# A postnorm layer with a routed mixture of experts on one core: the router's logits by four column groups, an earlier turn of y, one more root by bits, and ScalarE as the one that empties the shared expert's output

## What is computed

```python
def reference(x, ...):                       # x: 4 sequences of 1024 tokens of 128 values
    x = _layernorm(x + attn(x))              # a memory layer: cumulative sums of cos and sin features
    x = _layernorm(x + ffn(x))

def attn(x):
    ...                                      # den, num_re, num_im: cumsum over the 1024 positions
    y = silu(out_re * ... + out_im * ...)
    return y @ W_out

def ffn(x):                                  # flat: 4096 tokens
    logits = flat @ router_w.T               # 8 experts
    topk_p, topk_i = top_k(softmax(logits), 2)
    combine[...] = topk_p / topk_p.sum()
    for e in range(8):
        out += mlp(flat, w_fc[e], w_proj[e]) * combine[:, e]
    out += mlp(flat, shared_fc, shared_proj)     # mlp: square(relu(x @ w_fc.T)) @ w_proj.T, 512 wide
```

## Time and profile before

| | |
|---|---|
| median of 3 runs | 523.81 us (523.81 to 528.99) |
| the profiled execution | 521.17 us, of which the span of the trace 519.4 us |
| mean granted clock of TensorE | 0.963 of full speed |
| busy, of the span | PE 89%, DVE 70%, ACT 68%, POOL 56% |
| memory stage | to 232.5 us |
| dispatch stage | 232.5 to 350.2 us |
| routed stage | 350.2 to 494 us |
| POOL's 64 scatters | 234.2 to 342.4 us |

### The profile page before, as it was taken

One profiled execution on the slowest core, in us unless ns is written; L12 is line 12 of the kernel. 1 busy time (PEld: TensorE's weight loads), 2 busy tenths in 40 slices (PEclk: granted clock), 3 DMA queues, 4 the chain that ended last, 5 costly groups with the idle time before them and its releaser, 6 DMA issues.

```text
span 519.4 us, 7568 instructions
## 1 busy us (share of the span) xinstructions
PE 462.2 (89%) x2192; PEld 299.7 (58%) x2192; DVE 362.2 (70%) x843; ACT 354.0 (68%) x551; POOL 292.5 (56%) x248
## 2 busy tenths in 40 slices
PE   8897999999999988878597877869999999999984
PEld 4333344443333333446375655658999999899732
DVE  7887999999999999997667715354343334465246
ACT  3889799999999999816244625516767666566507
POOL 3473667877787778827565563521545455655400
PEclk9997999999999999999698987989999999999998
DMA  7031226664343433001111010121222221222095
GB/s 261 3 108 55 82 76 208 221 237 146 124 147 124 147 125 145 3 1 44 41 42 42 32 51 17 42 77 42 69 77 78 67 67 57 59 62 60 16 319 166
DMA packets 41192, 48.55 MB, mean 93 GB/s; under 512 B 5616, under 2 KB 25266, under 8 KB 41152
## 3 DMA queue, kind: packets, MB, share of 16 engines
q1 hardware_dynamic: 35792, 39.07, 23.0%
q0 software_dynamic: 5216, 8.70, 5.3%
q10 hardware_dynamic: 144, 0.31, 0.2%
HBM read 19.17 MB, written 29.11 MB: 93 GB/s over the span
## 4 chain that ended last, share of the span: by engine, by line
PE 36%; DVE 36%; issue 9%; ACT 8%; another core or an unknown queue 5%; POOL 3%; DMA 2%; DVEq 0%; SPq 0%; POOLq 0%; ACTq 0%
PE routed_ph L1438 13%; PE routed_po L1451 12%; DVE memory_y_raw L753 9%; DVE memory_prod L744 9%; DVE memory_feat L729 4%; PE memory_nsum L596 3%; POOL table_scratch L1129 2%; PE routed_px L1426 2%; ACT finish_xo L1645 2%; PE dispatch_spo L960 1%; ACT memory_feat L376 1%; PE dispatch_sph L950 1%; DVE dispatch_xrow L1197 1%; DMA finish_pick<-pick_scratch 1%
## 5 line engine op out<-in xcount | busy, mean ns | idle before, releaser
L479 POOL TENSOR_TENSOR memory_feat<-memory_feat,memory_p_tok 128x1024 f32<-128x1024 f32 x64 | 121.8, 1934 | 46.2 <-ACT memory_feat L387 45.2
L596 PE MATMUL memory_nsum<-memory_feat,tri 128*128 128x512 f32 x256 | 116.9, 599 | 6.6 <-ACT memory_last_rows L396 3.6
L1414 POOL DMA_INDIRECT pick_scratch<-routed_ob,routed_xg x71 | 71.3, 1005 | 78.0 <-DVE routed_ob L1535 57.7
L1129 POOL DMA_INDIRECT table_scratch<-dispatch_xrow,dispatch_slot x64 | 61.8, 966 | 47.9 <-DVE dispatch_slot L1232 25.8
L596 PEld LDWEIGHTS memory_nsum<-memory_feat,tri 128*128 128x128 f32 x256 | 47.5, 191 | 65.3 <-issue 54.5
L1484 ACT ACTIVATE routed_rel<-routed_ph 128x512 f32<-128x512 f32 x71 | 42.3, 597 | 47.5 <-PE routed_ph L1438 46.3
L1438 PE MATMUL routed_ph<-routed_xs,routed_w1c 128*128 128x256 f32 (+1 forms) x368 | 71.2, 337 | 2.1 <-ACT routed_xs L1475 1.3
L1451 PE MATMUL routed_po<-routed_w2c,routed_hid 128*128 128x128 f32 x568 | 71.2, 275 | 0.5 <-ACT routed_hid L1493 0.5
L1535 DVE TENSOR_SCALAR routed_ob<-routed_po,routed_xg 128x128 f32<-128x128 f32 x71 | 22.6, 348 | 68.9 <-issue 47.4
L744 DVE TENSOR_TENSOR memory_prod<-memory_nsum,memory_query 128x1024 f32<-128x1024 f32 x58 | 68.3, 1215 | 1.0 <-PE memory_nsum L596 1.0
L1451 PEld LDWEIGHTS routed_po<-routed_w2c,routed_hid 128*128 128x128 f32 x568 | 67.0, 192 | 0.9 <-ACT routed_hid L1493 0.7
(11 more groups left out here) (188 smaller groups left out, 652.8 us busy)
## 6 DMA issues: line engine op xcount, KB each, us to landing
table_scratch<-memory_blank SPq DMA_DIRECT2D x68, 260.0 KB, 2.6
finish_pick<-pick_scratch SPq DMA_DIRECT2D x16, 256.0 KB, 5.8
routed_xg<-table_scratch SPq DMA_DIRECT2D x25, 130.0 KB
w<-w_up SPq DMA_DIRECT2D x9, 256.0 KB, 2.7
w<-w_down SPq DMA_DIRECT2D x9, 256.0 KB, 3.2
x_tok<-x SPq DMA_DIRECT2D x4, 512.0 KB, 3.7
out<-finish_xo SPq DMA_DIRECT2D x7, 256.0 KB, 2.3
routed_xg<-table_scratch SPq DMA_DIRECT2D x21, 65.0 KB
```

Of the source, the lines that this page charges most:

```text
L479: nc.gpsimd.tensor_tensor(v, v, pv, ALU.mult).then_inc(wfeat_done, 1)
L596: last = nc.tensor.matmul(nsum[:, o:o + 512], tri[:], feat[:, i % U, h, q * 512:(q + 1) * 512], start=True, stop=True)
L1129: nc.gpsimd.indirect_dma_start(out=table, in_=xrow[:, r, n, :], in_offset=None, out_offset=bass.IndirectOffsetOnAxis(ap=slot[:, r, n:n + 1 ...
L1414: nc.gpsimd.indirect_dma_start(out=pick_dram, in_=ob[:, u, h, :], in_offset=None, out_offset=bass.IndirectOffsetOnAxis(ap=xg[:, t % XU, h, ...
```

## The change

Five edits.

- **Router.** For groups 1 to 7 the router's weights, padded with zeros from 8 to 32 columns, become the stationary side, once for each of four column groups of the PE array, and a tile of x is the moving side. The logits come out with the experts along the partitions (`plT`). ACT copies them to `lT` (new step `keep_l`, 128x128), PE turns them back by one transpose (new step `turn_l`) into `plt`, and `choose` reads them there. The logits of group 0 are made as before. The three views `plT`, `plt` and `pr` share one bank.
- **y sooner.** `turn_y(g+3)` moves from behind `up(g, 3)` to right behind `rank(g+1)`; `keep_y(g+3)` moves from ACT's end of the round to the place before `relu(g, 2)`.
- **First downs.** `down(0, 0)` and `down(0, 1)` move from ahead of `rank(1)` into round 1, where the other rounds have theirs.
- **Root of group 6** by bits instead of POW.
- **Shared output.** ACT copies `spo` to `y_all` (`keep_shared`, at the head of its round, groups 6 and 7 at the stage's end); the add of x is done on DVE in the routed stage, after tiles 6, 8, ... 20 (`add_input`), from SBUF. The finish waits for it (`summed`).

```diff
-POWERS = (0, 1, 2, 4, 6)
+POWERS = (0, 1, 2, 4)
...
-        routerT = sb("routerT", [P, E])
+        routerT = sb("routerT", [P, K])
...
+            nc.vector.memset(routerT[:, E:], 0.0)
...
-        pl, pr = plr[:, 0:GT * E], plr[:, GT * E:2 * GT * E + E]
+        plT, plt, pr = plr[:, 0:P], plr[:, P:2 * P], plr[:, 2 * P:2 * P + GT * E + E]
+        pl = plt.rearrange("p (t e) -> p t e", t=GT)[:, :, 0:E]
...
                 for t in range(GT):
-                    last = nc.tensor.matmul(pl[:, t * E:(t + 1) * E], x1T[:, g % XR, t, :], routerT[:],
-                                            start=True, stop=True)
-                last.then_inc(log_done, 1)
+                    if g:
+                        last = nc.tensor.matmul(plT[t * K:(t + 1) * K, :], routerT[:], x1T[:, g % XR, t, :],
+                                                start=True, stop=True)
+                    else:
+                        last = nc.tensor.matmul(pl[:, t, :], x1T[:, g % XR, t, :], routerT[:, 0:E], start=True, stop=True)
+                last.then_inc(routed_done if g else log_done, 1)
+
+            def turn_l(g):
+                pe.wait_ge(lT_kept, g)
+                nc.tensor.transpose(plt, lT[:], ident[:]).then_inc(log_done, 1)
...
                     up(g, 0)
                     if g + 1 < NG:
                         route(g + 1)
-                    if g > 1:
-                        down(g - 1, 0)
+                    down(g - 1, 0)
+                    if g + 1 < NG:
+                        turn_l(g + 1)
                     up(g, 1)
-                    if g > 1:
-                        down(g - 1, 1)
+                    down(g - 1, 1)
                     if g + 1 < NG:
                         rank(g + 1)
                     else:
                         total()
+                    if g + 3 < NG:
+                        turn_y(g + 3)
                     up(g, 2)
                     down(g - 1, 2)
                     up(g, 3)
-                    if g + 3 < NG:
-                        turn_y(g + 3)
                     down(g - 1, 3)
...
+            def keep_l(g):
+                act.wait_ge(routed_done, g)
+                nc.scalar.copy(lT[:], plT).then_inc(lT_kept, 1)
+
...
+            def keep_shared(g):
+                act.wait_ge(down_done, g + 1)
+                nc.scalar.copy(y_all[:, group(g), :].rearrange("p t c -> p (t c)"), spo[:]).then_inc(added, 1)
...
                 for g in range(NG):
+                    if g >= 2:
+                        keep_shared(g - 2)
                     if 0 < g < NG - 1:
                         keep_x(g + 1)
                     relu(g, 0)
+                    if 0 < g < NG - 1:
+                        keep_l(g + 1)
                     square(g, 0)
...
                         weigh(g + 1)
+                    if 0 < g and g + 3 < NG:
+                        keep_y(g + 3)
                     relu(g, 2)
...
-                    if g + 3 < NG:
-                        keep_y(g + 3)
+                    if g == 0:
+                        keep_y(3)
+                keep_shared(NG - 2)
+                keep_shared(NG - 1)
...
                 for g in range(NG):
-                    if g >= 2:
-                        add_shared(g - 2)
                     if g + 2 < NG:
                         residual(g + 2)
...
+            def add_input(g):
+                v = slice(g * GT, (g + 1) * GT)
+                dve.wait_ge(dis.added, g + 1)
+                nc.vector.tensor_tensor(y_all[:, v, :], y_all[:, v, :], xrow[:, 0, v, 0:D], ALU.add).then_inc(summed, 1)
...
+                if t in SUMMED_AT:
+                    add_input(SUMMED_AT.index(t))
...
+            pe.wait_ge(rou.summed, NG)
             shared(4)
```

More of the change, by code:

```diff
@@ L984, in rest @@
                 turn_x(1)
+                route(1)
                 up(0, 2)
-                route(1)
+                turn_l(1)
                 up(0, 3)
                 turn_y(3)
-                down(0, 0)
-                down(0, 1)
                 rank(1)
@@ L1232, in place @@
                 nc.vector.tensor_copy(slot[:, :, group(g)], spot[:]).then_inc(slot_done, 1)
-            def add_shared(g):
-                dve.wait_ge(down_done, g + 1)
-                nc.vector.tensor_tensor(y_all[:, group(g), :], spo[:].rearrange("p (t c) -> p t c", c=D),
-                                        xrow[:, 0, group(g), 0:D], ALU.add).then_inc(added, 1)
             def table_of_tiles():
```

25 lines of the change are left out of this document (15 added, 10 removed).

## The result

The changed kernel took **526.76 us** in the median of 4 runs (525.53 to 529.73), the kernel before 523.81 (516.09 to 528.99): ratio **1.0159**, 95% interval 1.0092 to 1.0225. So it is slower, by 1.6% on this measure and by 0.6% by the medians, where a gain of 0.9% was forecast.

The account below looks back on a forecast made before the run. Handoffs bound the dispatch stage, with PE's signals held during POOL's scatter bursts. Terms 0 - 0.8 - 3.5 + 0.1 - 0.4 gave -4.6 us, so 519.2 us (-0.9%), range 513 to 528.

Parts of the forecast that it names:

- my rule: Dispatch stage: PE's signals are held once POOL has scattered some 6 us, and come free 0.6 to 1.6 us after a pause.
- Router's path: Dispatch rounds: `choose` now waits for route, copy and transpose; with `residual` as cover the added wait costs 0 to 0.3 us.
- rival B: Dispatch rounds: the router's transposed logits fall into the hold, three rounds 2.5 us longer, +6.4 in all, 530 us; chance 0.16.
- Root of group 6: Rounds 4 and 5: without the POW's pause two joined bursts separate, the pair falling from 30.3 to 26.8 us: -3.5.
- The add off DVE: Round of 15.2 us, where DVE is the chain: -0.8 us; 0 in held rounds, and `add_input` costs 0 in the routed stage.
- Router on PE: Router's product in each dispatch round: -0.3 us of PE, tiling-mode drain some 0.3 a round at most; 0 in the sum.
- y sooner: Projections in the dispatch stage: their waits for `keep_y`, 1.48 and 0.41 us, both go; DVE or the held signal is late next.
- Start of the routed stage: First `up` of the routed stage no longer waits for weight copies behind DVE's last add: -0.4 us, between -0.86 and +0.1.

Follow-up runs that it names:

- e15: Changed kernel plus about 1.9 us of spare work on GpSimd before the fifth scatter of groups 1 to 6, signals late: 517.02 us, 0.9889 of before.
- e5: The changed kernel itself run again, on a chip where signals came late: 527.14 us, 1.0125 of the kernel before (1.0023 by the medians).
- e14: Changed kernel without the router's part, signals late: 518.94 us, 0.9943 of the kernel before.
- e13: Kernel before with the router's part alone, signals late: 522.07 us, 1.0008 of the kernel before.
- e3: Kernel before with only group 6's root taken from bits, no signal late: 496.66 us, 0.9980 of the kernel before.
- e17: Changed kernel with the POW of group 6 put back, signals late: 522.93 us, 1.0165 of the kernel before (0.9993 by the medians).
- e2: Kernel before with only the shared output's copies on ScalarE and late adds, no signal late: 497.61 us, 0.9994 of the kernel before.
- e12: The changed kernel itself, on a chip where no signal was late: 494.99 us, 0.9940 of the kernel before.
- e1: Changed kernel with the shared output added on VectorE as before, no signal late: 494.57 us, 0.9922 of the kernel before.
- e6: Changed kernel with the shared output added on VectorE as before, signals late: 530.82 us, 1.0205 of the kernel before (1.0093 by the medians).
- e10: Changed kernel without the router's part, no signal late: 494.52 us, 0.9934 of the kernel before.
- e8: Kernel before with only y turned sooner, signals late: 524.49 us, 1.0036 of the kernel before (0.9973 by the medians).
- e4: Kernel before with the router's part alone, no signal late: 497.70 us, 0.9995 of the kernel before.
- e9: Kernel before with the router's part alone, again with no signal late: 497.51 us, 1.0010 of the kernel before.
- e7: Changed kernel with two PSUM banks for the downs and copies at ScalarE's round end, signals late: 528.73 us, 1.0137 of the kernel before.

## Why the prediction was wrong

**The bound.** Right: handoffs bound the dispatch stage, and TensorE's signals come late while GpSimd scatters without a pause; e15 shows by intervention that work of another kind on GpSimd lets them out. Three things in my rule were wrong. It isn't the kernel's: on two chips no signal was late, and the same phase takes 88 us there. The lateness sets in sooner than the 5.5 to 6.5 us that I read: in e5 a product that ends 3.8 us into its burst (264.80, burst from 261.00) is read by ScalarE 1.9 us later, at 266.72, behind a "remote" wait of 1.65. And it isn't a hold until the pause: signals came 1.9 to 7.4 us late inside bursts that ran on (331.88 in e5, 336.03 in after). The 303.60 of the earlier trace rows, inside the double burst of 289.17 to 310.10, already says so.

**The step that failed: "Router's path", put at 0 to 0.3.** I had the logits ready 4.2 to 5.2 us into a burst, with `residual` as cover. In e5 they were ready at 5.3 to 6.4 (267.37, 280.15, 298.34, 314.05, 330.03 against bursts of 261.00 to 324.75), in three of the five because the product's own signal was late, and the transpose's signal then came 1.6 to 5.1 us late on top. Three rounds grew to 16.1 to 17.5 where I had 13.2. This is **rival B**, at 530 and 0.16, with its mechanism and its place; its +2.5 in three rounds was +2.9 to +4.3. Three things limit this. In the profile of the result the logits were ready 2.1 to 4.6 us into their bursts, no later than I had them, and `choose` still waited 5.6 us for them in all, so there the fault is that the signal was taken as prompt until 5.5 us; the larger loss of that execution is the last term below. That leaving the router out takes the loss away rests on e14, on a chip where the changed kernel was not run. And why the router alone costs nothing (e13, 1.0008) although its transposes come late too stays open: its profile, one execution, has a double burst of groups 2 and 3 and then a round of 18.0 us.

**"Root of group 6", -3.5, the largest term, failed as well.** It rested on one pair of rounds in one execution. Without late signals the root is worth 0.8 us, not clear of the noise (e3). With them, nothing of the 3.5 us can be seen when the POW is given back (e17, 0.9993 by the medians). Without this term my sum was -1.1, close to no change. The pause of a POW does let some signals out (268.93 in e5, 0.9 us after the end of the POW of 267.04), but in which rounds bursts run together is drawn anew in each execution: groups 4 and 5 in the profile of before, 2 and 3 (and 6 and 7) in that of after, none from group 2 on in e5.

**"The add off DVE", -0.8.** The sign is right and the size small: 0 without late signals (e2 alone; e12 against e1 by 0.2%), and with them the copies are 3.7 us quicker than the adds in the changed kernel (e5, e6). `add_input` in the routed stage costs nothing, as I had it.

**"Router on PE", -0.3 a round.** Measured without late signals, in e12 and then e10:

```profile
268.55 1.02 PE L962 MATMUL dispatch_sph<-dispatch_x1T,w 128*128 128x512 f32 x2
269.50 0.43 PE L927 MATMUL dispatch_plr<-dispatch_x1T,routerT 128*32 128x128 f32 x8
269.86 1.16 PE L972 MATMUL dispatch_spo<-w,dispatch_shid 128*128 128x128 f32 x8
270.85 0.27 PE L935 MATMUL dispatch_plr<-ident,dispatch_lT 128*128 128x128 f32 x1
270.96 1.02 PE L962 MATMUL dispatch_sph<-dispatch_x1T,w 128*128 128x512 f32 x2
```

```profile
271.99 1.02 PE L950 MATMUL dispatch_sph<-dispatch_x1T,w 128*128 128x512 f32 x2
272.85 0.97 PE L921 MATMUL dispatch_plr<-routerT,dispatch_x1T 128*128 128x8 f32 x8
273.68 1.14 PE L960 MATMUL dispatch_spo<-w,dispatch_shid 128*128 128x128 f32 x8
```

From the product's start to the next row's 0.36 instead of 0.83, and 0.11 for the transpose. But the `up` ahead of the product takes 0.95 from its start to the product's instead of 0.86, and the down behind it 0.99 instead of 0.97. Together 2.41 instead of 2.66: 0.25 saved. The Trainium skill, "TensorEngine Tiling (Array Packing)", Key Properties, has TensorE drained by a change of tiling mode. The trace agrees with some price at both edges of the product, 0.09 ahead of it and 0.02 behind it, against my estimate of 0.3 a round; that the drain makes it was not isolated.

**"y sooner".** Alone it is within the noise where signals are late (e8, 1.0036). Without late signals I never ran it alone; since the router, the root and the copies are worth 0, 0.8 and 0 there, and the changed kernel 2.5, y should be worth 1 to 2 us. That is argued, not shown.

**"Start of the routed stage", -0.4.** The term itself held: the first `up` no longer waits for VectorE (359.58 has no idle time; the earlier trace rows had 0.86), and from the end of TensorE's last downs to it are 1.3 us instead of 2.0. But my sum took GpSimd's last scatter for what releases the stage. In the profile of after it was TensorE's backlog, which ended 17 us behind that scatter, and the stage started 7.4 us later than before. The earlier trace rows had this already: the downs of 344.80 run to 350.2, where the stage ends, 8 us behind the last scatter. TensorE's wait for the last copies and its backlog are a term that the sum left out, and in this execution it is larger than all the others.

**A near hit that is luck.** My sum and the case without late signals differ little (-0.9% forecast, -0.6% measured in e12), but that is luck: the terms that made it were others.

## What to carry to other kernels

Where a profile has waits that end "remote" on a kernel of one core, look for the engine that is busy without a pause at that time, and time the kernel on more than one chip before judging a change: here the change gained 0.6% in one set of runs and gained nothing or lost in the two others. A further handoff in a chain can cost not its own length but the delay of a late signal: the shorter product of the router, with one signal more, was level where it stood alone (e4, e9, e13), and the version of the change without it was quicker than the kernel before in both kinds of sets (e10, e14). And a term that rests on which rounds ran together in one execution is a draw, not a cost.

## What the runs showed of the hardware

- In four of the six sets signals of TensorE are read late while GpSimd issues indirect scatters back to back, 0.96 us each with 0.30 between: by 1.4 us for a product over 3.7 us into its burst (278.1 in e5), by up to 14 us for the downs of a double burst (over at 329.5, read at 343.76 in after). When GpSimd turned to other work they came out together, 0.9 and 1.2 us after it began (e15). Some came through in the middle of a burst, 2.6 and 7.4 us late (298.65 and 336.03 in after). What delays them stays open: no run looked into that.
- It goes with the set of runs, and each set of experiments had its own chip; whether it belongs to the chip or to something else that differed then is open. Four sets had it, the result's among them (kernel before at 522.6 to 525.9 us, spread of 12 to 17), two had none (497.5, spread of 3 to 5). GpSimd's scatters last the same in both, and the first starts at 233.2 to 234.7 us in every profile.
- The mean granted clock was 0.956 to 0.960 in e5 to e7 and 0.976 in e12. In after it was 0.50 of full speed, the lower of its two levels, from 277 to 286 us, behind an idle 5.32 us of TensorE, and the transpose of 283.60 lasts 0.48 us there, against 0.27 in e12. That is a part of the lost time; its size was not measured.
